# One core, one decoder block: the first loads merged and reordered, the row scale moved from the products to the down weight, and the last products reordered

## The chip, the core and the metric

The program runs on one core of one Trainium2 chip. The metric is the device time of one execution, in microseconds (us). The core has five engines that run side by side: TensorE (PE in the profile; PEld is its weight load), VectorE (DVE), ScalarE (ACT), GpSimd (POOL) and SyncE (SP), which here only issues DMA transfers. Data lies in SBUF (128 partitions); TensorE writes its sums to PSUM, here eight banks of 512 floats per partition.

## The reference

The input x is 4 batches of 256 tokens of 256 numbers. Three steps, each with a residual:

```python
x = x + linear_attention(layernorm(x))      # 16 heads of 16; q, k, v, o with biases; elu + 1
x = x + softmax_scores(ctx, ctx, layernorm(x), masks)   # (ctx Wq+bq)(ctx Wk+bk)^T/8 * layernorm(x), masked, softmax
x = x + ffn(layernorm(x))
# ffn:  y = fwht(x * SU_ug);  h = silu(y W_gate^T * ws_gate) * (y W_up^T * ws_up)
#       h = fwht(h * SU_dp);  out = h W_down^T * Wscale_dp
```

`fwht` is a normalised Hadamard transform over the last dimension; ctx is 4 x 256 x 64. The softmax of the second step is added to x itself, as its 256 columns are the 256 numbers of a token. `Wscale_dp` scales the 256 columns of the result, and since h W_down^T is linear in W_down, it can be put on the products or on the weight.

## The kernel before

**Tiles.** x lies in `x_res` (name `xs`) as 8 tiles of 128 tokens, two for each batch b. A factor that needs more than the short format of TensorE is split into a high part (a cast on ACT, functions `..._hi`) and a low part (a subtraction on DVE or POOL, `..._lo`), and one product is three passes: low by high, high by high, high by low.

**The start.** TensorE first runs `WARM` products of zeros (`junk`), then `mx` (the 65 x 65 product of the context weights), `u` (mx by the transposed context, in two halves), `T1` (the turn of the first batch's normalised x against the unit matrix), `SC` 0 (context scores of batch 0), and then K, V and Q of batch 0. The order is the list `HEAD`. x0 needs on its way to `T1`: statistics (`ln_stats` on DVE), `rstd_of` on POOL, `normalise1` on DVE; after `T1` comes `xT_hi` on ACT, at which K starts, and `xT_lo` on DVE. Each projection has a bias product of its own at its end; `bias_lo` on DVE makes the low part, and Q waits at its start for the second call.

**Masks.** The two masks' bytes are loaded, added on POOL (`mask_sum`), and spread to `mbias` on ACT (L396). The bytes lie in the buffer `at`, which `attend(0)` (L742) writes; `attend(0)` waits for `mbias` (L738).

**The feed-forward part.** For batch b and block j of 128 of the 1024 inner numbers, `gate_up` makes gate and up (L1123, 12 products); ACT takes silu (L521), DVE multiplies (`hidden`, L822), ACT and POOL split (L530, L311). `SIDE` says after which block of a batch the work for later batches is put in: `WD` 0 to 3 are the Hadamard products over the down weight, `XH` that over x. `down(b)` (L1136) sums both tiles of a batch over the eight blocks: first blocks 0 to 6 of tile 0, then of tile 1, then the last block of each. `add_y` on DVE scales the sum by `Wscale_dp` in PSUM (L833) and adds it to x (L835); SP then stores the tile.

**Banks.** Seven banks are handed out in turn, in the order of the groups. A group waits until its bank's last owner was read (`bank_read`). `XH` 1 takes the bank of `WD` 0, `GU` 6 that of `WD` 1, and the two sums of `down(0)` those of `WD` 2 and 3.

**Queues.** All loads but three are issued by SP in the order of the program, those three (context weights, unit matrix, bias rows) by ACT. Each engine does its own list strictly in order, and waits with the whole list behind it.

## Time and profile before

| | us |
|---|---|
| median of 3 runs | 138.21 |
| lowest, highest | 137.3, 138.31 |
| profiled execution | 135.21 |
| its span, first to last instruction | 133.4 |
| granted TensorE clock in it, mean | 0.998 |
| PE busy (share of the span) | 125.2 (94%) |
| DVE, ACT, POOL busy | 80.9, 75.8, 71.0 |

The profiled execution is 1.8 us longer than its span, and 3.0 us shorter than the median of the runs. All rows below are from it; times in them count from the start of the span. Instructions that read one list are read as: start, length, engine, line, operation, what it writes <- what it reads, how many; in brackets how long the engine was idle before it and what ended that.

### The profile page before, as it was taken

What the parts mean: (1) busy time and instruction counts of PE and PEld (TensorE: products, weight loads), DVE (VectorE), ACT (ScalarE), POOL (GpSimd) and SP (SyncE); (2) the same over time, 40 slices, a digit from 0 to 9 for tenths busy, and PEclk for the clock granted to TensorE, in tenths of its full rate; (3) what the DMA queues carried; (4) which work ended last, traced back from release to release, by engine and by line L of the source; (5) the groups of instructions that cost most, each with busy time, mean ns of one, the idle gap of its engine ahead of it and who ended that gap; (6) DMA issues with size and microseconds to landing.
All of it is one profiled execution on the core that took longest, in us unless ns stands there. A gap on an engine that the chain in (4) does not pass through costs nothing.

```text
span 133.4 us, 2624 instructions
## 1 busy us (share of the span) xinstructions
PE 125.2 (94%) x975; PEld 116.9 (88%) x975; DVE 80.9 (61%) x205; ACT 75.8 (57%) x162; POOL 71.0 (53%) x90
## 2 busy tenths in 40 slices
PE   6989797999899999999999999999999999999980
PEld 2249696999899999889999989999989999999980
DVE  0269985789986895857786696564635413324122
ACT  4168579595676589568543982654397530355300
POOL 3015999959999998855270352650226440144600
PEclk9999999999999999999999999999999999999999
DMA  3899976000000000000000200000200000200002
GB/s 69 231 387 374 396 244 227 5 0 2 2 5 0 0 2 5 0 0 0 5 0 0 79 0 5 2 0 0 82 1 0 2 0 5 79 0 0 5 0 79
DMA packets 4721, 7.64 MB, mean 57 GB/s; under 512 B 608, under 2 KB 2592, under 8 KB 4580
## 3 DMA queue, kind: packets, MB, share of 16 engines
q1 hardware_dynamic: 4478, 7.37, 16.1%
q10 hardware_dynamic: 230, 0.11, 0.5%
q8 instruction: 8, 0.13, 0.4%
q14 instruction: 5, 0.04, 0.1%
HBM read 6.42 MB, written 1.05 MB: 56 GB/s over the span
## 4 chain that ended last, share of the span: by engine, by line
PE 76%; DVE 6%; DMA 4%; SPq 3%; POOL 3%; ACT 2%; issue 2%; POOLq 0%; DVEq 0%
PE bank L1123 35%; PE bank L1136 17%; PE bank L1001 5%; PE bank L1087 4%; DMA at<-in_mask_key 4%; PE bank L1025 3%; PE bank L1109 3%; PE bank L1049 2%; PE bank L1059 2%; PE bank L1095 1%; PE bank L1069 1%; ACT mbias L396 1%; POOL at L280 1%; PE bank L992 1%; DVE st L647 1%
## 5 line engine op out<-in xcount | busy, mean ns | idle before, releaser
L1123 PE MATMUL bank<-xh_home,wug 128*128 128x256 f32 x384 | 49.5, 285 | 0.0
L1123 PEld LDWEIGHTS bank<-xh_home,wug 128*128 128x128 f32 x384 | 47.2, 190 | 0.5 <-issue 0.4
L311 POOL TENSOR_TENSOR hs<-front,hs 128x256 fp32r<-128x256 f32 x32 | 24.1, 761 | 32.6 <-ACT hs L530 32.6
L521 ACT ACTIVATE front<-bank,vecs 128x256 f32<-128x256 f32 x32 | 15.0, 473 | 18.6 <-PE bank L1123 18.5
L822 DVE SCALAR_TENSOR_TENSOR front<-bank,sc_up,front 128x256 f32<-128x256 f32 x32 | 15.2, 480 | 16.1 <-ACT front L521 16.1
L1136 PE MATMUL bank<-wdh,hs 128*128 128x256 f32 x192 | 23.8, 283 | 0.0
L1136 PEld LDWEIGHTS bank<-wdh,hs 128*128 128x128 f32 x192 | 23.4, 191 | 0.1
L530 ACT CAST hs<-front 128x256 fp32r<-128x256 f32 x32 | 12.8, 400 | 5.5 <-DVE front L822 5.4
L1025 PE MATMUL bank<-wqkv,xT 128*128 128x256 f32 x96 | 14.2, 289 | 0.0
L1025 PEld LDWEIGHTS bank<-wqkv,xT 128*128 128x128 f32 x96 | 12.3, 189 | 0.6 <-DVE xT L689 0.4
L647 DVE BATCH_NORM_STATS2 st<-x_res 128x6 f32<-128x256 f32 x24 | 9.1, 416 | 5.2 <-DMA x_res<-in_x 5.0
L258 POOL TENSOR_SCALAR veps<-mv 128x2 f32<-128x2 f32 x12 | 2.3, 193 | 16.0 <-DVE mv L650 15.3
L300 POOL TENSOR_TENSOR wd_b<-wd_a 128x1024 f32<-128x1024 f32 x4 | 10.0, 2509 | 0.1
L260 POOL TENSOR_TENSOR rstd<-veps,mhalf 128x2 f32<-128x2 f32 x12 | 8.5, 708 | 1.0
L833 DVE TENSOR_TENSOR bank<-bank,rows 128x256 f32<-128x256 f32 x8 | 3.4, 424 | 8.9 <-PE bank L1136 8.8
L1049 PE MATMUL bank<-xT,wqkv 128*128 128x256 f32 x48 | 7.1, 286 | 0.0
L1087 PE MATMUL bank<-wo,aT 128*128 128x256 f32 x48 | 6.5, 284 | 0.0
L1049 PEld LDWEIGHTS bank<-xT,wqkv 128*128 128x128 f32 x48 | 6.3, 190 | 0.0
L961 PE MATMUL bank<-back 128*128 128x512 bf16 x11 | 5.1, 629 | 1.3 <-POOL back L314 1.3
L1087 PEld LDWEIGHTS bank<-wo,aT 128*128 128x128 f32 x48 | 6.0, 190 | 0.0
L486 ACT ACTIVATE bank<-bank,low 128x256 f32<-128x256 f32 x8 | 3.6, 444 | 4.2 <-DVE low L775 4.2
L288 POOL TENSOR_TENSOR x_res<-x_res,rows 128x512 f32<-128x512 f32 x4 | 5.2, 1296 | 0.0
(105 smaller groups left out, 194.9 us busy)
## 6 DMA issues: line engine op xcount, KB each, us to landing
wd_a<-in_w_d SPq DMA_DIRECT2D x1, 1024.0 KB, 8.6
front<-in_w_ug SPq DMA_DIRECT2D x2, 512.0 KB, 9.8
back<-in_w_ug SPq DMA_DIRECT2D x2, 512.0 KB, 5.3
out<-x_res SPq DMA_DIRECT2D x8, 128.0 KB, 1.9
wd_b<-in_w_qkv SPq DMA_DIRECT2D x3, 256.0 KB, 5.6
x_res<-in_x SPq DMA_DIRECT2D x1, 512.0 KB, 6.8
back<-in_ctx_t SPq DMA_DIRECT2D x1, 260.0 KB
x_res<-in_x SPq DMA_DIRECT2D x2, 128.0 KB, 3.3
```

The costliest lines, as they stand in the source:

```text
L260: g.tensor_tensor(rstd[:, n - 1, two], veps[:, n - 1, two], mhalf[:, 0:2], ALU.pow).then_inc(s[f"rstd{n}"], 1)
L300: g.tensor_tensor(dst[:, :, half, :], src[:, :, 0, :], src[:, :, 1, :], ALU.subtract if half else ALU.add)\
L311: g.tensor_tensor(hs[:, 1, n % JB, :], sg[:, n % RING, :], hs[:, 0, n % JB, :].bitcast(F32), ALU.subtract)\
L521: a.activation(sg[:, n % RING, :], B("GU", n)[:, 0:SEQ], ACT.Silu, scale=vecs[:, V_WSUG + JB + j:V_WSUG + JB + j + 1]).then_inc(s["sg"], 1)
L530: a.copy(hs[:, 0, n % JB, :], sg[:, n % RING, :]).then_inc(s["h_hi"], 1)
L647: v.bn_stats(st[:, n - 1, t, :], xs[:, t, :]).then_inc(s[f"stats{n}"], 1)
L822: v.scalar_tensor_tensor(sg[:, n % RING, :], B("GU", n)[:, SEQ:2 * SEQ], sc_up[:, j:j + 1], sg[:, n % RING, :], ALU.mult, ALU.mult).then_i ...
L1025: ins = mm(into, xT[:, b % 2, xb, k, i * P:(i + 1) * P], wqkv[:, wa, c, k, :], start=(n == 0), stop=(name == "V" and n == len(X_PASSES) - 1))
L1049: mm(into, wqkv[:, wa, 2, k, m * P:(m + 1) * P], xT[:, b % 2, xb, k, :], start=(n == 0), stop=False)
L1087: ins = mm(dst[:, i * HID:(i + 1) * HID], aT[:, ab, k, i * P:(i + 1) * P], wo[:, wa, k, :], start=(n == 0), stop=(n == len(X_PASSES) - 1))
L1123: ins = mm(dst[:, n * SEQ:(n + 1) * SEQ], wug[:, wa, k, at_col + j * P:at_col + (j + 1) * P], xh[b][:, xb, k, :], start=(i == 0), stop=(i ...
L1136: ins = mm(dst[i][:, 0:HID], hs[:, hb, j, i * P:(i + 1) * P], wdh[:, wa, j, :], start=(j == 0 and n == 0), stop=(j == JB - 1 and n == 2))
```

## The change

The change has these parts:

- **First loads.** The unit matrix stands ahead of x in one array, and both share the buffer `x_res`; the first load brings it with both tiles of batch 0 (320 KB; before, two loads of 128 KB and one of 64 KB). The context weights stand behind the context in one array and come with it in the second load (293 KB, before 260 and 32.5 KB). The bias load on ACT's queue no longer waits for a memset on POOL. On SP's queue the row vectors and masks move up, and `vecs` moves down.
- **Bias rows.** Three rows instead of 65; they are negated, as is the row of ones that they are multiplied with.
- **Order at the start.** `WARM` is 8 instead of 9; `T1` comes between the two halves of `u`; `SC` 0 comes after Q. On ACT `xT_hi` and `exp_k` come earlier, on POOL `rstd_of(1, 1)` comes ahead of `ctx_lo(0)`, on DVE `xT_lo` comes ahead of `bias_lo` and `u_lo`, and `ln_stats(1, 1)` ahead of the second `bias_lo`.
- **Masks' bytes** lie in the buffer `score` instead of `at`. The wait of `attend(0)` for `mbias` stays in the code.
- **Down weight.** `wd_scale` on DVE multiplies the four `WD` groups by `Wscale_dp` in PSUM, ahead of `wd_hi` and `wd_lo`; `add_y` has one instruction per tile instead of two.
- **Last batch.** `down(3)` ends tile 0 after two blocks of tile 1; six blocks of tile 1 follow.

```diff
 BANKS = 8
-WARM, WARM_MORE = 9, 2
+WARM, WARM_MORE = 8, 2
...
-HEAD = (("mx", 0), ("u", 0), ("u", 1), ("T1", 0), ("SC", 0), ("K", 0), ("V", 0), ("Q", 0), ("T1", 1), ("ST", 0),
+HEAD = (("mx", 0), ("u", 0), ("T1", 0), ("u", 1), ("K", 0), ("V", 0), ("Q", 0), ("SC", 0), ("T1", 1), ("ST", 0),
...
-        xs = sb("x_res", [P, TILES, HID])
+
+        first = sb("x_res", [P, P + TILES * HID])
+        ident, xs = first[:, 0:P], first[:, P:].rearrange("p (t d) -> p t d", d=HID)
...
-        wx = sb("wx", [CTX, 2 * CTX1])
...
-        ctxT = back[0:CTX1, 0, :]
-        junk = back[:, 1, 0:CHUNK // 2].bitcast(BF16)
+        ctx_raw = back[0:CTX1, :, :].rearrange("p i c -> p (i c)")[:, 0:TOK + 2 * CTX1]
+        ctxT, wx = back[0:CTX1, 0, :], back[0:CTX, 1, 0:2 * CTX1]
...
-        bytes_of = at[:, :, :, :].rearrange("p two i d -> p (two i d)").bitcast(U8)
...
+        bytes_of = score[:, :, :].rearrange("p b s -> p (b s)").bitcast(U8)
...
         @block.sync
         def _(sp):
-            sp.dma_start(xs[:, 0:1, :], x[:, 0:1, :]).then_inc(ld["x0"], 16)
-            sp.dma_start(xs[:, 1:2, :], x[:, 1:2, :]).then_inc(ld["x1"], 16)
-            sp.dma_start(ctxT, ctx_t).then_inc(ld["ctx"], 16)
+            sp.dma_start(first[:, 0:P + ST * HID], x[:, 0:P + ST * HID]).then_inc(ld["x0"], 16)
+            sp.dma_start(ctx_raw, ctx_t).then_inc(ld["ctx"], 16)
             sp.dma_start(qkv_raw[:, 0], w_qkv[:, 0]).then_inc(ld["wk"], 16)
             sp.dma_start(qkv_raw[:, 1], w_qkv[:, 1]).then_inc(ld["wv"], 16)
             sp.dma_start(qkv_raw[:, 2], w_qkv[:, 2]).then_inc(ld["wq"], 16)
-            sp.dma_start(xs[:, 2:4, :], x[:, 2:4, :]).then_inc(ld["x2"], 16)
-            sp.dma_start(xs[:, 4:8, :], x[:, 4:8, :]).then_inc(ld["x3"], 16)
-            sp.dma_start(vecs[:, :], vec).then_inc(ld["vec"], 16)
+            sp.dma_start(first[:, P + ST * HID:P + 2 * ST * HID], x[:, P + ST * HID:P + 2 * ST * HID]).then_inc(ld["x1"], 16)
+            sp.dma_start(rows[:, 0:2, :], row[0:2, :].partition_broadcast(P)).then_inc(ld["row"], 16)
             sp.dma_start(mss, mask_ss).then_inc(ld["mss"], 16)
             sp.dma_start(mkey, mask_key.partition_broadcast(P)).then_inc(ld["mkey"], 16)
-            sp.dma_start(cst[:, P:], const[:, P:]).then_inc(ld["cst"], 16)
+            sp.dma_start(first[:, P + 2 * ST * HID:], x[:, P + 2 * ST * HID:]).then_inc(ld["x2"], 16)
+            sp.dma_start(cst[:, :], const).then_inc(ld["cst"], 16)
             sp.dma_start(wo_raw, w_o).then_inc(ld["wo"], 16)
-            sp.dma_start(rows[:, 0:2, :], row[0:2, :].partition_broadcast(P)).then_inc(ld["row"], 16)
+            sp.dma_start(vecs[:, :], vec).then_inc(ld["vec"], 16)
             sp.dma_start(wd_a[:, :, :], w_d).then_inc(ld["wd"], 16)
             for n, c in enumerate(UG_ORDER):
                 if n == 2:
                     sp.wait_ge(s["ctx_lo"], 2)
-                    wait_full(sp, "K", 0)
+                    wait_full(sp, "SC", 0)
                 sp.dma_start(stage[n], w_ug[:, :, c * CHUNK:(c + 1) * CHUNK]).then_inc(ld[f"ug{n}"], 16)
             sp.dma_start(rows[:, 2:3, :], row[2:3, :].partition_broadcast(P)).then_inc(ld["wsd"], 16)
...
             g.memset(junk, 0.0).then_inc(s["junk"], 1)
-            g.memset(bias_raw, 0.0).then_inc(s["bias_zero"], 1)
             g.memset(mhalf[:, :], -0.5)
...
             pool.wait_ge(s["xn1"], 2)
             mask_sum()
-            pool.wait_ge(s["w_lo"], 3)
-            ctx_lo(0)
             rstd_of(1, 1)
             shift_of(1, 1)
+            ctx_lo(0)
             ctx_lo(1)
             rstd_of(1, 2)
             shift_of(1, 2)
...
-            act.dma_start(wx[:, :], w_x).then_inc(ld["wx"], 16)
-            act.dma_start(cst[:, 0:P], const[:, 0:P]).then_inc(ld["ident"], 16)
+            act.dma_start(bias_home[:, 0:2 * HID + 1], bias).then_inc(ld["bias"], 16)
...
-                act.dma_start(bias_raw[ROW_HI:BIAS_ROWS:ROW_LO, :], bias).then_inc(ld["bias"], 16)
+            def minus_ones():
+                a.copy(minus[:, :], neg1[0:BIAS_ROWS, :].to_broadcast([BIAS_ROWS, HID])).then_inc(s["minus"], 1)
...
             def wd_hi(n):
-                wait_full(act, "WD", n)
+                act.wait_ge(s["wd"], n + 1)
...
-            bias_rows()
+            minus_ones()
             mx_copy()
             bias_hi(K_COLS)
             w_hi("wk", 0)
             u_copy()
+            xT_hi(0)
             u_hi(0)
-            xT_hi(0)
             w_hi("wv", 1)
             w_hi("wq", 2)
             bias_hi(Q_COLS)
+            exp_k(0)
             u_hi(1)
-            exp_k(0)
             ctx_hi(0)
             ctx_hi(1)
...
             def bias_lo(n, cols):
-                low_row = slice(ROW_LO, ROW_LO + 1)
+
                 dve.wait_ge(s["bias_hi"], n + 1)
-                v.tensor_tensor(bias_r[low_row, cols], bias_raw[low_row, cols], bias_r[low_row, cols].bitcast(F32), ALU.subtract)\
-                    .then_inc(s["bias"], 1)
+                v.scalar_tensor_tensor(bias_r[:, cols], bias_r[:, cols].bitcast(F32), bias_low, bias_raw[:, cols],
+                                       ALU.mult, ALU.subtract).then_inc(s["bias"], 1)
...
+            def wd_scale(n):
+
+                wait_full(dve, "WD", n)
+                if n == 0:
+                    dve.wait_ge(ld["wsd"], 16)
+                w = B("WD", n)[:, :].rearrange("p (j o) -> p j o", o=HID)
+                v.tensor_tensor(w, w, rows[:, 2:3, :].to_broadcast([P, WDP, HID]), ALU.mult).then_inc(s["wd"], 1)
...
             def add_y(b):
-
-                if b == 0:
-                    dve.wait_ge(ld["wsd"], 16)
                 for i in range(ST):
                     t = ST * b + i
                     wait_full(dve, "Y", b, i)
-                    y = B("Y", b, i)[:, 0:HID]
-                    v.tensor_tensor(y, y, rows[:, 2, :], ALU.mult).then_inc(s["y"], 1)
-                    dve.wait_ge(s["y"], t + 1)
-                    v.tensor_tensor(xs[:, t, :], y, xs[:, t, :], ALU.add).then_inc(read_of("Y", b, i), 1)
+                    v.tensor_tensor(xs[:, t, :], B("Y", b, i)[:, 0:HID], xs[:, t, :], ALU.add).then_inc(read_of("Y", b, i), 1)
 
             ln_stats(1, 0)
             normalise1(0)
             w_lo(0)
+            xT_lo(0)
             bias_lo(0, K_COLS)
             u_lo(0)
-            xT_lo(0)
             w_lo(1)
             w_lo(2)
+            ln_stats(1, 1)
             bias_lo(1, Q_COLS)
-            ln_stats(1, 1)
             elu_k(0)
             v_add(0)
             u_lo(1)
@@ -895,9 +894,13 @@
             hidden(2)
             x3_lo(1)
             hidden(3)
+            wd_scale(0)
+            wd_scale(1)
+            hidden(4)
             wd_lo(0)
             wd_lo(1)
-            hidden(4)
+            wd_scale(2)
+            wd_scale(3)
             at_lo(2)
...
-                pe.wait_ge(ld["wx"], 16)
+                pe.wait_ge(ld["ctx"], 16)
...
-                    pe.wait_ge(ld["ctx"], 16)
...
-                if b == 0:
-                    pe.wait_ge(ld["ident"], 16)
...
+                if b == BATCH - 1:
+
+                    for j in range(JB - 1):
+                        pe.wait_ge(s["h_lo"], JB * b + j + 1)
+                        block_products(0, j)
+                    block_products(1, 0)
+                    block_products(1, 1)
+                    pe.wait_ge(s["h_lo"], JB * b + JB)
+                    done(block_products(0, JB - 1), "Y", b, 0)
+                    for j in range(2, JB - 1):
+                        block_products(1, j)
+                    done(block_products(1, JB - 1), "Y", b, 1)
+                    return
...
-        "x": blocks(a["x"].reshape(TOK, HID)),
-        "ctx_t": np.concatenate([a["ctx_512"].reshape(TOK, CTX).T, np.ones((1, TOK), np.float32)]),
+        "x": np.concatenate([np.eye(P, dtype=np.float32), blocks(a["x"].reshape(TOK, HID)).reshape(P, -1)], 1),
+        "ctx_t": np.concatenate([np.concatenate([a["ctx_512"].reshape(TOK, CTX).T, np.ones((1, TOK), np.float32)]),
+                                 np.concatenate([w_x, np.zeros((1, 2 * CTX1), np.float32)])], 1),
         "w_qkv": np.stack([blocks(a[n].T) for n in ("L0_attn_k_w", "L0_attn_v_w", "L0_attn_q_w")], 1),
-        "bias": np.stack([b_kq, b_kq, np.ones(2 * HID, np.float32)]),
+        "bias": np.concatenate([np.stack([b_kq, b_kq, np.ones(2 * HID, np.float32)]), np.array([[0], [1], [0]], np.float32)], 1),
```

The change moves instructions in three places that matter here. **TensorE, from the start to the first K product**, before (bank: a PSUM bank; wx, mx, back, eq: context weights, their product, the home of the context, the first u; cst and x_res: where the unit matrix is):

```order
L961 MATMUL bank<-back 128x512 x9
L966 MATMUL bank<-wx 65x65
L961 MATMUL bank<-back 128x512 x2
L974 MATMUL bank<-back,mx 65x512 x2
L1001 MATMUL bank<-cst,xn 128x128 x4
L989 MATMUL bank<-eq,back 128x256 x2
L1025 MATMUL bank<-wqkv,xT 128x256 x6
L1031 MATMUL bank<-bias_r,ones 128x256
L1025 MATMUL bank<-wqkv,xT 128x256 x6
L1031 MATMUL bank<-bias_r,ones 128x256
```

And now:

```order
L964 MATMUL bank<-back 128x512 x8
L969 MATMUL bank<-back 65x65
L964 MATMUL bank<-back 128x512 x2
L976 MATMUL bank<-back,mx 65x512
L1003 MATMUL bank<-x_res,xn 128x128 x4
L976 MATMUL bank<-back,mx 65x512
L1025 MATMUL bank<-wqkv,xT 128x256 x6
L1031 MATMUL bank<-bias_r,minus 128x256
```

The two products of L989 (`SC` 0) are gone from here (they stand behind Q), one half of `u` stands behind the turn, and one warming product is left out.

**VectorE, from the first weight's low part to `elu_k(0)`**, before (wqkv: weights; hs here: the low part of u; st, mv: statistics of x):

```order
L685 TENSOR_TENSOR wqkv<-wd_b,wqkv 128x512
L661 TENSOR_TENSOR bias_r<-kvs,bias_r 1x256
L670 TENSOR_TENSOR hs<-bank,hs 65x256
L689 TENSOR_TENSOR xT<-bank,xT 128x512
L685 TENSOR_TENSOR wqkv<-wd_b,wqkv 128x512 x2
L661 TENSOR_TENSOR bias_r<-kvs,bias_r 1x256
L647 BN_STATS st<-x_res 128x6 x2
L650 BN_AGGR mv<-st 128x2 x2
L698 SCALAR_TENSOR_TENSOR kp<-ek,bank 128x512
```

And now:

```order
L682 TENSOR_TENSOR wqkv<-wd_b,wqkv 128x512
L686 TENSOR_TENSOR xT<-bank,xT 128x512
L658 SCALAR_TENSOR_TENSOR bias_r<-bias_r,kvs 3x256
L667 TENSOR_TENSOR hs<-bank,hs 65x256
L682 TENSOR_TENSOR wqkv<-wd_b,wqkv 128x512 x2
L644 BN_STATS st<-x_res 128x6 x2
L647 BN_AGGR mv<-st 128x2 x2
L658 SCALAR_TENSOR_TENSOR bias_r<-bias_r,kvs 3x256
L695 SCALAR_TENSOR_TENSOR kp<-ek,bank 128x512
```

The turned x comes first, and the statistics of the second batch stand ahead of the second bias row.

**VectorE in the first batch's feed-forward part, from `hidden(3)` on**, before (front: the hidden blocks; wdh: the split down weight; rows: the row vectors), with what each waits for:

```order
L822 SCALAR_TENSOR_TENSOR front<-bank,sc_up,front 128x256 [waits s_sg]
L813 SCALAR_TENSOR_TENSOR wdh<-bank,wdh 128x512 [waits s_wd_hi] x2
L822 SCALAR_TENSOR_TENSOR front<-bank,sc_up,front 128x256 [waits s_sg]
L679 TENSOR_TENSOR aT<-bank,aT 128x512 [waits s_at_hi]
L813 SCALAR_TENSOR_TENSOR wdh<-bank,wdh 128x512 [waits s_wd_hi] x2
L822 SCALAR_TENSOR_TENSOR front<-bank,sc_up,front 128x256 [waits s_sg]
```

And now:

```order
L827 SCALAR_TENSOR_TENSOR front<-bank,sc_up,front 128x256 [waits s_sg]
L813 TENSOR_TENSOR bank<-bank,rows 128x512 [waits ld_wsd,bank_full0]
L813 TENSOR_TENSOR bank<-bank,rows 128x512 [waits bank_full1]
L827 SCALAR_TENSOR_TENSOR front<-bank,sc_up,front 128x256 [waits s_sg]
L818 SCALAR_TENSOR_TENSOR wdh<-bank,wdh 128x512 [waits s_wd_hi] x2
L813 TENSOR_TENSOR bank<-bank,rows 128x512 [waits bank_full4]
L813 TENSOR_TENSOR bank<-bank,rows 128x512 [waits bank_full5]
L676 TENSOR_TENSOR aT<-bank,aT 128x512 [waits s_at_hi]
L818 SCALAR_TENSOR_TENSOR wdh<-bank,wdh 128x512 [waits s_wd_hi] x2
L827 SCALAR_TENSOR_TENSOR front<-bank,sc_up,front 128x256 [waits s_sg]
```

Four instructions on the banks of `WD` are new, and `hidden(4)` stands ahead of the first two low parts instead of behind them.

## Rows read from the trace of the kernel before

**Rows 1.** The waits of PE over the whole span: in total, times, longest, us.

```profile
PE bank L1001 <- DVE at L742: 1.1, 1, 1.1
```

**Rows 2.** Timeline, TensorE up to 11 us: start, length, what.

```profile
1.30 4.02 PE L961 MATMUL bank<-back 128*128 128x512 bf16 x9 [1.30 <-POOL back L314]
...
5.25 0.48 PE L966 MATMUL bank<-wx 64*65 64x65 f32 x2
5.66 1.03 PE L961 MATMUL bank<-back 128*128 128x512 bf16 x2
...
7.05 1.90 PE L974 MATMUL bank<-back,mx 65*65 65x512 f32 x4 [0.36 <-DMA back<-in_ctx_t]
...
8.79 0.60 PE L1001 MATMUL bank<-cst,xn 128*128 128x128 f32 x4
10.07 1.23 PE L1025 MATMUL bank<-wqkv,xT 128*128 128x256 f32 x6
```

**Rows 3.** Timeline, two DMA issues at the start.

```profile
0.72 0.57 ACTq L374 DMA_DIRECT2D wx<-in_w_x  x1
...
1.16 0.42 SPq L223 DMA_DIRECT2D x_res<-in_x  x1
```

**Rows 4.** DMA issues of the start; the last number is us to landing.

```profile
x_res<-in_x SPq DMA_DIRECT2D x1, 128.0 KB, 4.3
...
wx<-in_w_x ACTq DMA_DIRECT2D x1, 32.5 KB, 3.6
```

**Rows 5.** Timeline, VectorE and TensorE from 9 to 18 us.

```profile
9.15 0.41 DVE L661 TENSOR_TENSOR bias_r<-kvs,bias_r 1x256 fp32r<-1x256 f32 x1
...
10.05 0.69 DVE L689 TENSOR_TENSOR xT<-bank,xT 128x512 fp32r<-128x512 f32 x1
...
10.66 1.28 DVE L685 TENSOR_TENSOR wqkv<-wd_b,wqkv 128x512 fp32r<-128x512 f32 x2
...
11.97 0.84 DVE L661 TENSOR_TENSOR bias_r<-kvs,bias_r 1x256 fp32r<-1x256 f32 x1
...
13.52 0.88 PE L1049 MATMUL bank<-xT,wqkv 128*128 128x256 f32 x6
...
13.73 0.66 DVE L698 SCALAR_TENSOR_TENSOR kp<-ek,bank 128x512 f32<-128x512 f32 x1
...
16.27 0.84 PE L1001 MATMUL bank<-cst,xn 128*128 128x128 f32 x4 [0.91 <-ACT xn L432]
...
17.90 1.17 PE L1025 MATMUL bank<-wqkv,xT 128*128 128x256 f32 x6
```

**Rows 6.** Timeline, first batch's feed-forward stage, 58 to 64 us.

```profile
58.61 1.08 ACT L511 ACTIVATE wdh<-bank 128x512 fp32r<-128x512 f32 x2
...
59.23 1.29 DVE L813 SCALAR_TENSOR_TENSOR wdh<-bank,wdh 128x512 fp32r<-128x512 f32 x2 [0.97 <-ACT wdh L511]
59.98 1.20 PE L1109 MATMUL bank<-x3T,had_x 128*128 128x256 f32 x8
...
61.87 0.69 DVE L679 TENSOR_TENSOR aT<-bank,aT 128x512 fp32r<-128x512 f32 x1 [0.96 <-ACT aT L465]
...
63.67 0.47 DVE L822 SCALAR_TENSOR_TENSOR front<-bank,sc_up,front 128x256 f32<-128x256 f32 x1
```

**Rows 7.** Timeline, the turn of `at` 3 in the second batch's stage.

```profile
78.72 0.63 PE L1001 MATMUL bank<-cst,at 128*128 128x128 f32 x4 [0.26 <-issue]
```

**Rows 8.** The chain of waits, its step before the fourth batch's turn.

```profile
98.99 0.12 issue
```

**Rows 9.** Timeline, the end of the program.

```profile
123.72 5.92 PE L1136 MATMUL bank<-wdh,hs 128*128 128x256 f32 x48
...
124.77 1.44 POOL L311 TENSOR_TENSOR hs<-front,hs 128x256 fp32r<-128x256 f32 x2 [0.70 <-ACT hs L530]
...
129.32 0.43 DVE L833 TENSOR_TENSOR bank<-bank,rows 128x256 f32<-128x256 f32 x1 [4.41 <-PE bank L1136]
...
130.59 0.42 DVE L835 TENSOR_TENSOR x_res<-bank,x_res 128x256 f32<-128x256 f32 x1
```

More of the change, by code:

```diff
@@ L86, in schedule, with decoder_kernel @@
     return [g for g in order if g not in (("SC", 0, 0), ("SC", 1, 0))]
-def decoder_kernel(nc, x, ctx_t, w_qkv, bias, w_o, w_x, w_ug, w_d, vec, row, mask_ss, mask_key, const, out):
+def decoder_kernel(nc, x, ctx_t, w_qkv, bias, w_o, w_ug, w_d, vec, row, mask_ss, mask_key, const, out):
     bank_of, turn_of = {}, {}
@@ L113, in decoder_kernel @@
         bias_r = sb("bias_r", [BIAS_ROWS, 2 * HID], F32R)
-        ones = sb("ones", [BIAS_ROWS, HID], F32R)
-        cst = sb("cst", [P, 2 * P + FB * SW])
-        ident, had, diag_mask = cst[:, 0:P], cst[:, P:2 * P], cst[:, 2 * P:]
+        minus = sb("minus", [BIAS_ROWS, HID], F32R)
+        cst = sb("cst", [P, P + FB * SW])
+        had, diag_mask = cst[:, 0:P], cst[:, P:]
         mbias = sb("mbias", [P, TILES, SEQ], BF16)
```

31 lines of the change are left out of this document (14 added, 17 removed).

## The prediction

> **What bounds the kernel now.** I read the page first: TensorE is busy for 94% of the span and its clock stands at 1.00 on average, so a gain has to come from the start, from the few places where TensorE waits, or from what follows its last product. The list of waits by engine gives one wait in the middle of the first stage of 1.1 us, for `at` of the first batch [rows 1]. The timeline gives the others: before the warming products 1.30, before `u` 0.36, before the turn of the second batch 0.91 [rows 2, 5], before the turn of `at` 3 0.26, and 0.12 in the chain of waits at 98.99 [rows 7, 8]. After the last product come four instructions of VectorE and a store [rows 9]. About 1% (1.4 us) is what a measurement of this kernel can tell from no change.
>
> **First loads and the order of the start.** Let L be the landing of the load that brings the context and its weights. Now `mx` waits for it; before, `mx` had its own small load, and only `u` waited for the context, to 7.05 [rows 2]. From L on TensorE has `mx` 0.41 (5.25 to 5.66), two warming products 0.86, half of `u` 0.87 (7.05 to 8.79 is two), `T1` 0.44 (four of 128 columns at the cost per column of `u`), and the other half of `u` 0.87: K starts at L + 3.45. The other path to K, from the start of `T1` over `xT_hi`, took 1.28 (8.79 to 10.07) [rows 2] and is as long as `T1` and half a `u`, 1.31.
>
> L is in no row. From below: the small load of context weights landed 3.6 after its issue at 0.72, so 4.32. From above: the context alone ended the wait at 7.05. I take the load that stood second on SP's queue, as this one will: issued at 1.16, landed 4.3 later, at 5.46 [rows 2 to 4]. The new load is larger, but there is now one load in front of it on the queue and one beside it on ACT's, instead of three beside it. K then starts at 8.91 instead of 10.07. Of x I ask only that it land before the context, since it is ahead of it.
>
> The second load of the old queue speaks to a rule. It was 128 KB and took 4.3 us [rows 4]. The Trainium skill, DMA: Bandwidth & Descriptors, in the part on the fixed and the variable cost, gives about 2.0 us and the bytes at 436 GB/s, which is 2.3 us; the row disagrees by 2 us. By that rule both first loads together (613 KB) would have landed at about 4.2 us (an estimate from that page), K would start at 7.6, and the sum below would end 1.3 us lower.
>
> **From K to the second batch's turn.** Before, Q started 3.45 after K, and the turn 6.20 after K, of it 0.91 as a wait for the normalised x [rows 2, 5]. The reordered list of VectorE puts a wait ahead of Q: from `xT_lo`, which starts with K, come `xT_lo` 0.61, `bias_lo` and `u_lo` 0.90 (9.15 to 10.05), two `w_lo` 1.31 (to 11.97), the statistics of the second batch 0.92 (12.81 to 13.73) and `bias_lo` 0.46, sum 4.20 [rows 5]. Q waits at its start for that second `bias_lo`, so it starts 4.20 after K and not 3.45. Then come its 14 products at 0.12 (six in 0.88, of which the last one's length is 0.28), 1.68, and `SC` 0 at 0.87 (as many columns as half of `u`). The turn starts 6.75 after K, at 15.66, without a wait for x: the statistics end 3.7 after K, which leaves 3.0 for the way over POOL and ACT, and before it took 2.5 (13.73 to 16.27). Before it was 16.27. From the turn to the next K product I keep 1.63 (16.27 to 17.90), since `exp_q` waited for its place behind x before and waits for `SC` 0 now. **The start brings -0.61**; with L from 4.32 to 7.05 it is -1.75 to +0.98. The second `bias_lo` took 0.84 beside POOL's mask sum [rows 5]; if it does so again, 0.4 is lost.
>
> **Bias rows, queue order, warming product.** The bias products have as many columns as before and the low part as many elements per partition: nothing. The load of masks moves up two places on SP's queue, the scale vectors down by four, and they are read by VectorE only after 15 us; the load of the later halves of `w_ug` waits for `ctx_lo`, which now comes behind `rstd_of`, and for `SC` 0, and is not needed before the first feed-forward stage: nothing. The ninth warming product ended before 5.4, and TensorE would now wait for L anyway: nothing, unless its clock minds.
>
> **Masks' bytes.** They leave the buffer that `attend(0)` writes, but `attend(0)` still waits for `mbias`. The 1.1 us [rows 1] stay: nothing. The same edit with the wait gone would be worth up to that.
>
> **Down weight.** VectorE was free at 58.26 (0.97 before 59.23) and started `hidden(5)` at 63.67. Now it has eight instructions of 512 columns at 0.60 from start to start (one of `L813`'s pairs is 1.29 long with an overlap), `at_lo` 0.61 and `hidden(4)` 0.40, sum 5.81: `hidden(5)` starts at 64.07, 0.40 later. `XH` 1 takes the bank of `WD` 0 and waits for its low part, which now ends at 60.54 (58.26, two scales 1.20, `hidden(4)` 0.40, and the low part's own length 0.68), where TensorE was ready at about 60.14 (its row begins at 59.98, before the end of the product in front of it) [rows 6]. So TensorE loses 0.40 there, and VectorE's list is 0.40 late as well, which runs on through the scores of batch 2 to the turn of `at` 3 at 78.72, where TensorE already waits 0.26 for it [rows 7]: **+0.40**, once. If the scale hides, it is 0; if PSUM to PSUM is slower than that pair (0.68 and not 0.60 for four), +0.7.
>
> **`add_y`.** It loses one of two instructions per tile. In the first and third batch they stand where VectorE waits anyway: nothing. In the second they stand ahead of `ln_stats(3, 3)`, and 0.8 less there takes away the 0.12 [rows 8]: **-0.12**.
>
> **The end.** The last 48 products are the same number. Tile 0 now ends 18 products (18 x 0.12 = 2.2) before the last, so its sum and store are over before tile 1 is ready. The wait for the last low part comes after 27 products instead of 42, at 123.9 + 3.2 = 127.1; POOL had it at 126.2 [rows 9], so there is no new wait. Behind the last product stands one instruction of 0.42 instead of the chain from 129.32 to 131.01 (1.69): **-1.25** after 0.02 for the semaphore.
>
> **Sum.** -0.61 + 0.40 - 0.12 - 1.25 = -1.58, against the profiled 135.21: 133.6. The median of the runs is 3.0 above that execution; the terms carry over: 138.21 - 1.58 = **136.6**.
>
> **Rivals.**
>
> *The loads stream* (0.23). With one request on ACT's queue instead of three, the first loads come without a pause, and L is the 4.32 of the smallest load: 1.14 earlier, 135.5. For it: the second load's 4.3 us for 128 KB shows that bytes were not its limit. Against it: nothing shows what the limit was.
>
> *The context comes late* (0.14). L is 7.05 as before. Then `mx` and the warming products, which lay before it, lie behind it, and the start is 0.98 later instead of 0.61 earlier: 138.2, no change. For it: the load is 32 KB larger than the one that landed then.
>
> *TensorE is slow when the work comes* (0.19). The warming products took 4.02 for nine of 512 columns, 0.43 each, the 1.2 GHz level, though the clock column says 1.00; the two at 5.66 took 1.03, the same level; Q's took 0.12 for 256 columns, the 2.4 GHz level [rows 2, 5]. Before the rise the engine had been busy with a gap of less than 0.4. Now it works to 4.7 and then waits to L. The Trainium skill, TensorE: Matmul & The Clock Gate, Part 1, says that the engine starts throttled and that activity releases it; the rows agree. If the rise comes only after the second half of `u`, that costs 0.87 + 0.44 + 0.87 = 2.18, of which the wait of Q takes 0.7: 138.1 (0.08). If it comes after V, the 26 products of K and V take 0.21 instead of 0.12, 2.4 more: 136.6 + 2.18 + 2.4 - 0.7 = **140.5, slower** (0.11). It decides from the point where the clock is still low at K. For it: the runs of this kernel differ from the profiled one by 3 us. Against it: the same kind of activity is there, only with a gap of 0.8.
>
> **How the numbers follow.** The forecast has 0.44, with its own spread of 0.7 either way (the bias row's 0.4, the scale's 0 to 0.7); 1% below 138.21 is 136.83, which leaves 0.27 of it faster and 0.17 the same. Faster: 0.27 + 0.23 = 0.50. Same: 0.17 + 0.14 + 0.08 = 0.39. Slower: 0.11. The range goes from 135.2, the streaming loads with the scale partly hidden, to 138.9, the late context with the slower scale and bias row; outside lie the slow clock and a little of the streaming case.
>
> **What would show it.** The first K product at 8.9 (L + 3.45), Q held by `bias_lo` for 0.7, the second turn at 15.7 with no wait on ACT, `at` still held by `mbias`, `XH` 1 held by a `WD` low part for 0.4, tile 0's sum over before the last product, and 0.4 between the last product and the last store's issue. L above 6.1 or products of 256 columns at 0.21 after K has begun would make it wrong.

## The result: slower, and the profile after

| | before | after |
|---|---|---|
| median of 4 runs, us | 138.26 | 141.84 |
| lowest, highest | 137.3, 138.31 | 140.81, 142.29 |
| profiled execution, its span | 135.21, 133.4 | 142.07, 140.3 |

By the medians the changed kernel is 3.6 us (2.6%) slower. Over all its runs the kernel before has two groups of times, near 135.5 and near 138.5; the comparison takes the lower one, near 135.6, and so gives a ratio of 1.046 [1.042, 1.050]. The changed kernel has one group. The forecast was 136.6, faster.

The start in the timeline of TensorE, after:

```profile
1.29 3.59 PE L964 MATMUL bank<-back 128*128 128x512 bf16 x8 [1.29 <-POOL back L316]
5.42 0.48 PE L969 MATMUL bank<-back 64*65 64x65 f32 x2 [0.54 <-DMA back<-in_ctx_t]
...
6.66 1.92 PE L976 MATMUL bank<-back,mx 65*65 65x512 f32 x2
8.36 1.06 PE L1003 MATMUL bank<-x_res,xn 128*128 128x128 f32 x4
...
10.14 2.27 PE L1025 MATMUL bank<-wqkv,xT 128*128 128x256 f32 x6
...
12.85 1.65 PE L1025 MATMUL bank<-wqkv,xT 128*128 128x256 f32 x6
14.43 0.58 PE L1031 MATMUL bank<-bias_r,minus 3*128 3x256 f32 x1
...
19.58 0.98 PE L1049 MATMUL bank<-xT,wqkv 128*128 128x256 f32 x6
...
21.77 0.60 PE L1003 MATMUL bank<-x_res,xn 128*128 128x128 f32 x4
```

The load of context and weights ended the wait at 5.42, as forecast (5.46). But everything until 19.6 runs at the 1.2 GHz level: half of `u` took 1.7 (6.66 to 8.36), where two halves took 1.74 before [rows 2], and the second six of K take 1.58 (12.85 to 14.43) where six of Q took 0.72 before (13.52 [rows 5] to 14.24). TensorE does not wait once from 5.42 to 19.6: 14 us of unbroken products at the lower level. The clock column says 1.00 all the same (view by windows: the length of the stretch; busy time and, in brackets, number of instructions of PE, PEld, DVE, ACT and POOL; then clock, DMA share and GB/s):

```profile
6.00:10.00 4.00, 4.00 (x9) 1.78 (x8) 1.43 (x3) 1.87 (x6) 0.05 (x1) 1.00 1.05 276
```

In these 4 us TensorE was busy throughout with 9 products. K starts at 10.14 (before 10.07) and the second batch's turn at 21.77 (before 16.27).

The second thing is in the bias products, and it is there at the high clock as well. The chain of waits of the kernel before, K's products of a later batch (start, length, what):

```profile
40.07 0.12 PE bank L1031
40.20 0.72 PE bank L1025 x6
```

The same products in the chain of waits after:

```profile
47.43 0.31 PE bank L1031
47.74 0.90 PE bank L1025 x6
```

A bias product over 3 rows has the 256 columns of one over 65, and holds the engine for 0.31 instead of 0.12; the six behind it take 0.90 instead of 0.72. Where the 0.19 and the 0.18 come from, the weight loads show. Before (timeline of PEld, start and length of each load):

```profile
39.80 0.19 PEld L1031 LDWEIGHTS bank<-bias_r,ones 65*128 65x128 f32 x1
39.91 0.79 PEld L1025 LDWEIGHTS bank<-wqkv,xT 128*128 128x128 f32 x6
```

After:

```profile
47.36 0.18 PEld L1031 LDWEIGHTS bank<-bias_r,minus 3*128 3x128 f32 x1
47.67 0.77 PEld L1025 LDWEIGHTS bank<-wqkv,xT 128*128 128x128 f32 x6
```

The load is as long (0.18 against 0.19), but before it began 0.11 ahead of its product, at 39.91 in the timeline, under the product in front of it. After, it begins at 47.36 together with its own product's row, and the load of the product behind begins 0.31 later and not 0.11. The rows in front of the two loads end at 47.43 and 47.74, so by the profile, which models these ends, neither load lies under another product but for 0.07. The Trainium skill, TensorEngine Tiling (Array Packing), Key Properties, says that a change of the tiling mode, which that page ties to the number of rows (128, 64 or 32), drains TensorE; these rows agree with a drain on either side of the product over 3 rows, and do not show the mode itself.

Of the rest, the list of waits by engine says:

```profile
PE bank L1003 <- DVE at L739: 1.0, 1, 1.0
```

`attend(0)` still holds TensorE, as forecast (1.1 before [rows 1]). And the end of the chain of waits:

```profile
131.71 5.77 PE bank L1136 x48
...
137.51 0.42 DVE x_res L834
```

One instruction of 0.42 follows the last product, which ends at 137.48. Before, the chain of 1.69 [rows 9] did not start there. The chain of waits of the kernel before has, in front of it:

```profile
123.89 5.42 PE bank L1136 x45
```

VectorE started at 129.32, behind the 45th of the 48 products, when the sum of tile 0 was ready; the last product ended at 129.64 (126.72 and 2.92 in the timeline), and 1.37 stood behind it, up to 131.01. After, the same distance is 0.45 (137.48 to 137.93).

**The 6.9 us between the two spans, by stretches of the profiled executions:** to the first K product +0.07; from there to the turn of the second batch +5.43 (11.63 against 6.20: low clock and four bias products); to the first K product of the second batch +0.04; from there to the first gate product +3.29 (32.11 against 28.82: twelve bias products at the high clock); from there to the end -1.93 (84.75 against 86.68), where the forecast had +0.40 - 0.12 - 1.25 = -0.97.

### The profile page after: what moved, and what is told of

Same layout as the page of the kernel before. It is cut to its first block, busy times and chain, and to the rows that moved or that the text cites. A ratio compares the mean times of both kernels' runs of the same rounds, so it can differ in the third digit from the quotient of the medians.

```text
span 140.3 us, 2611 instructions
## 1 busy us (share of the span) xinstructions
PE 134.4 (96%) x974; PEld 122.6 (87%) x974; DVE 79.4 (57%) x201; ACT 76.0 (54%) x162; POOL 72.0 (51%) x89
## 4 chain that ended last, share of the span: by engine, by line
PE 90%; DMA 3%; ACT 3%; issue 1%; DVE 1%; SPq 0%; DVEq 0%; ACTq 0%
PE bank L1123 33%; PE bank L1136 16%; PE bank L1025 10%; PE bank L1049 5%; PE bank L1087 4%; PE bank L1003 4%; DMA back<-in_ctx_t 3%; PE bank L1109 3%; PE bank L976 2%; PE bank L1069 2%; PE bank L1059 2%; PE bank L1031 2%; PE bank L1050 2%; PE bank L994 2%; PE bank L1095 1%; ACT mbias L393 1%
## 5 line engine op out<-in xcount | busy, mean ns | idle before, releaser
L1025 PE MATMUL bank<-wqkv,xT 128*128 128x256 f32 x96 | 17.7, 334 | 0.1
L1025 PEld LDWEIGHTS bank<-wqkv,xT 128*128 128x128 f32 x96 | 14.6, 223 | 2.5 <-issue 1.3
L1049 PE MATMUL bank<-xT,wqkv 128*128 128x256 f32 x48 | 8.2, 309 | 0.0
L834 DVE TENSOR_TENSOR x_res<-bank,x_res 128x256 f32<-128x256 f32 x8 | 3.1, 419 | 8.8 <-PE bank L1136 8.7
L1049 PEld LDWEIGHTS bank<-xT,wqkv 128*128 128x128 f32 x48 | 6.8, 206 | 0.6 <-issue 0.2
L447 ACT ACTIVATE ek<-bank,neg 128x512 f32<-128x512 f32 x4 | 2.7, 687 | 7.4 <-PE bank L1031 7.4
L456 ACT ACTIVATE eq<-bank,neg 128x512 f32<-128x512 f32 x4 | 2.8, 690 | 6.4 <-PE bank L991 3.4
L964 PE MATMUL bank<-back 128*128 128x512 bf16 x10 | 4.6, 628 | 1.3 <-POOL back L316 1.3
```

What stands on the lines that cost most here:

```text
L1025: ins = mm(into, xT[:, b % 2, xb, k, i * P:(i + 1) * P], wqkv[:, wa, c, k, :], start=(n == 0), stop=(name == "V" and n == len(X_PASSES) - 1))
L1049: mm(into, wqkv[:, wa, 2, k, m * P:(m + 1) * P], xT[:, b % 2, xb, k, :], start=(n == 0), stop=False)
```

## The experiments

The theories. *Bias rows*: the product over 3 rows costs more in itself, against "columns alone count", on which the forecast rested. *Clock*: the first 20 us run at 1.2 GHz because of what TensorE does in the first five; within it, either the pause of 0.54 ahead of `mx` decides or the amount of work. The rest of the change is worth what the forecast said for it. All times are medians if nothing else is said, "before" stands for the kernel before on the same chip, and the medians of different groups come from different chips.

### First group: bias rows and warming, apart and together

Before here: 136.85 (135.33 to 139.38, 10 runs).

**a_bias65**: the change with its bias block zeroed to 65 rows, three of them loaded.

```diff
-BIAS_ROWS = 3
+BIAS_ROWS = 65
...
+            g.memset(bias_home[:, 0:2 * HID + 1], 0.0).then_inc(s["bias_zero"], 1)
...
+            act.wait_ge(s["bias_zero"], 1)
-            act.dma_start(bias_home[:, 0:2 * HID + 1], bias).then_inc(ld["bias"], 16)
+            act.dma_start(bias_home[0:3, 0:2 * HID + 1], bias).then_inc(ld["bias"], 16)
```

> The changed kernel with 65 bias rows instead of 3 (62 of them zeros, written by POOL ahead of the load). Theory R (a product over 3 rows takes 0.31 us and the one behind it 0.19 more, where 65 rows took 0.12): the pair of six products and a bias product falls from 1.11 to 0.84, 16 times 0.28 is 4.4 us, so the span falls from 140.3 to about 136. Theory C (the low clock alone explains the time, rows do not matter): no change.

Measured: 136.06 (132.65 to 136.87, 4 runs). Timeline of TensorE:

```profile
12.59 1.30 PE L1027 MATMUL bank<-wqkv,xT 128*128 128x256 f32 x6
13.72 0.28 PE L1033 MATMUL bank<-bias_r,minus 65*128 65x256 f32 x1
13.84 1.57 PE L1027 MATMUL bank<-wqkv,xT 128*128 128x256 f32 x12
```

At 65 rows the product holds the engine for 0.12 again (13.72 to 13.84). The clock is still late, rising within the six from 12.59 on. The times spread over 4 us: three runs took 135.5 to 136.9, and one 132.65, less than every run of a_bias65_warm10 below, so by its time the clock was early in it.

**a_warm10**: the change with ten warming products ahead of `mx`.

```diff
-WARM, WARM_MORE = 8, 2
+WARM, WARM_MORE = 10, 2
```

> The changed kernel with 10 warming products instead of 8, so that TensorE works until 5.5 us and the pause of 0.54 before the product of the context weights is gone. Theory C (that pause keeps the clock low until 19.6): halves of u at 0.87 instead of 1.71, K's products at 0.12 instead of 0.21, span 4 to 5 us lower, about 136. Rival (the moment of the rise is not tied to the pause): at most 0.2 us of difference, products at 0.21 still behind 15 us.

Measured: 136.37 (136.03 to 136.8, 6 runs), ratio 1.006 [1.003, 1.009]. Timeline of TensorE:

```profile
1.29 4.45 PE L964 MATMUL bank<-back 128*128 128x512 bf16 x10 [1.29 <-POOL back L316]
...
6.47 1.02 PE L976 MATMUL bank<-back,mx 65*65 65x512 f32 x2
7.33 0.60 PE L1003 MATMUL bank<-x_res,xn 128*128 128x128 f32 x4
...
8.60 1.23 PE L1025 MATMUL bank<-wqkv,xT 128*128 128x256 f32 x6
9.76 0.38 PE L1031 MATMUL bank<-bias_r,minus 3*128 3x256 f32 x1
10.08 0.97 PE L1025 MATMUL bank<-wqkv,xT 128*128 128x256 f32 x6
```

Half of `u` takes 0.86, the 2.4 GHz level, and K starts at 8.60. The ten products take 4.45 and `mx` follows without a pause. By the medians two more products of zeros bring 5.5 us, and one group of times. The bias product still takes 0.32 (9.76 to 10.08) and the six behind it 0.90.

**a_bias65_warm10**: both edits.

> Both: 65 bias rows and 10 warming products. R and C together: 131.5 to 132.5 of span, below the kernel before. R alone: as with 65 rows alone, about 136. C alone: as with 10 warming products alone.

Measured: 133.44 (133.24 to 133.72, 4 runs), ratio 0.985 [0.982, 0.988]: 1.5% below the kernel before. At 65 rows and early clock the parts of the change pay. The bias rows cost 136.37 - 133.44 = 2.9 where the clock is high, and 141.84 - 136.06 = 5.8 by the medians with eight warming products. Timeline of TensorE:

```profile
1.29 3.72 PE L966 MATMUL bank<-back 128*128 128x512 bf16 x10 [1.29 <-POOL back L316]
5.58 0.33 PE L971 MATMUL bank<-back 64*65 64x65 f32 x2 [0.57 <-DMA back<-in_ctx_t]
...
8.41 1.23 PE L1027 MATMUL bank<-wqkv,xT 128*128 128x256 f32 x6
...
12.35 0.94 PE L1051 MATMUL bank<-xT,wqkv 128*128 128x256 f32 x6 [0.22 <-issue]
...
15.65 0.84 PE L1005 MATMUL bank<-x_res,xn 128*128 128x128 f32 x4 [0.54 <-ACT xn L431]
```

Here a pause of 0.57 stands ahead of `mx`, as long as the 0.54 of the change, and the clock is high behind it. But it had risen before the pause: the ten products took 3.72, where the same ten took 4.45 in a_warm10.

**b_bias3**: the kernel before with the three bias rows of the change, and nothing else of it.

```diff
-ROW_HI, ROW_LO, ROW_ONE, BIAS_ROWS = 0, 32, 64, 65
+BIAS_ROWS = 3
...
```

> The kernel before with 3 bias rows (negated, with the row of -1 factors), nothing else changed. R: 4.4 us slower than before, ratio about 1.032. C or any other cause: within 0.3 us of before.

Measured: 141.5 (139.15 to 144.47, 4 runs), ratio 1.031 [1.023, 1.039]. By the medians this one part makes the old kernel 4.7 us slower, by the ratio 4.2. Its profiled execution (144.47) shows the low clock too:

```profile
7.56 3.65 PE L974 MATMUL bank<-back,mx 65*65 65x512 f32 x4 [0.87 <-DMA back<-in_ctx_t]
```

The same four products took 1.90 in [rows 2]; the work in front of them, nine warming products, `mx` and two more, is the same in both and took the same time. What differs is the pause behind it, 0.87 here and 0.36 there.

### Second group: what the other parts are worth

Here the base is a_bias65_warm10 (133.44), with high clock and 65 rows; before on this chip: 137.71 (135.3 to 139.66, 7 runs).

**m_free_at**: `attend(0)` no longer waits for `mbias` (the scores do, further on).

```diff
                 dve.wait_ge(s["z_inv"], b + 1)
-                if b == 0:
-                    dve.wait_ge(s["mbias"], 1)
```

> The kernel with 65 bias rows and 10 warming products, and with the wait of attend(0) for mbias taken out, which the move of the masks' bytes allows (at and the bytes share no memory any more). Theory M (the wait is all that held at): the wait of TensorE before the turn of at, 1.15 us in the kernel with both, falls to 0.4 or less, and the span by 0.7 to 1.1, to about 130.5. Rival (the wait only moves: logits(0) needs mbias too, and the chain through VectorE over the scores sets the time): the turn comes earlier, the span stays at 131.4 within 0.3.

Measured: 132.22 (131.94 to 132.71, 4 runs), ratio 0.972 [0.962, 0.983]; against the base -1.2, and -0.9 by the spans (130.5 and 131.4). The list of waits by engine no longer has the wait for `at`, 1.2 in the base. This is the fastest version of the study, 2.8% below the kernel before by the ratio and 4.0% by the medians of its chip. In the base, which has the masks' bytes moved and the wait kept, TensorE still waits 1.15; the move pays only with this line gone.

**m_old_tail**: the last batch summed in the old order.

```diff
-                if b == BATCH - 1:
-
-                    for j in range(JB - 1):
...
-                    done(block_products(1, JB - 1), "Y", b, 1)
-                    return
```

> The kernel with 65 bias rows and 10 warming products, with the last batch's products in the old order. Theory T: both tiles are ready together, and two additions of 0.42 stand behind the last product instead of one, so it is 0.4 us slower (the rest of the forecast 1.25 belongs to the scale that left add_y). Rival (the store of tile 0 delays that of tile 1 as well): 0.8 or more.

Measured: 133.25 (133.06 to 133.7, 4 runs), no difference to the base that these runs can tell, where 0.4 more was expected; the spans are 131.6 and 131.4. The end of the chain of waits:

```profile
122.86 5.42 PE bank L1138 x45
128.27 0.02 issue
128.29 0.78 DVE x_res L836 x2
```

And of the base:

```profile
122.89 5.77 PE bank L1138 x48
...
128.69 0.42 DVE x_res L836
```

In the old order VectorE starts behind the 45th product, in the new one behind the 48th. The two additions end at 129.07 and the one at 129.11. So with the scale on the weight the new order of the sums brings nothing.

**m_old_scale**: the scale back in `add_y`, the down weight unscaled.

```diff
-            wd_scale(0)
-            wd_scale(1)
-            hidden(4)
             wd_lo(0)
             wd_lo(1)
-            wd_scale(2)
-            wd_scale(3)
+            hidden(4)
             at_lo(2)
...
-                    v.tensor_tensor(xs[:, t, :], B("Y", b, i)[:, 0:HID], xs[:, t, :], ALU.add).then_inc(read_of("Y", b, i), 1)
+                    v.tensor_tensor(y, y, rows[:, 2, :], ALU.mult).then_inc(s["y"], 1)
+                    dve.wait_ge(s["y"], t + 1)
+                    v.tensor_tensor(xs[:, t, :], y, xs[:, t, :], ALU.add).then_inc(read_of("Y", b, i), 1)
```

> The kernel with 65 bias rows and 10 warming products, with the row scale in add_y as before and no wd_scale. Theory S (forecast): 0.45 more behind the last product, 0.3 to 0.4 less in the first batch's feed-forward part (XH 1 waits 0.3 in the kernel with both), 0.12 more before the fourth batch's turn: 0.2 slower, within 0.2. Rival (the four scales cost VectorE's chain 1 us or more): 0.5 faster or more.

Measured: 134.12 (133.56 to 134.42, 4 runs), 0.7 slower than the base, where 0.2 was expected; span 132.2. Chain of waits:

```profile
59.49 1.04 PE bank L1104 x8
...
98.31 0.12 issue
98.43 0.84 PE bank L998 x4
99.27 2.87 PE bank L1118 x24
...
129.00 0.44 DVE bank L831
...
129.47 0.43 DVE x_res L833
```

And the chain of waits of the base:

```profile
59.83 1.21 PE bank L1111 x8
...
98.53 0.44 PE bank L1005 x4
98.96 2.87 PE bank L1125 x24
```

Without the scale on the weight, `XH` 1 starts at 59.49 and without a wait, so the scale costs the base 0.34 there. At the turn of the fourth batch the base is 0.22 behind (98.53 against 98.31). Behind it the base is 0.31 ahead (98.96 against 99.27): the wait of 0.12 is gone, and the four products take 0.44 instead of 0.84. At the end (128.69 in the base) it is ahead by another instruction of 0.44 and its start.

**w_rows64**: the base with 64 bias rows, one run. 

> The kernel with both, but 64 bias rows. Question: from what number of rows does a bias product cost 0.12 instead of 0.31? If what counts is that the product uses less than the whole height, 64 rows would cost as 3 do (0.31, and 0.90 for the six behind it) and the span would be about 134.5; if only a height of at most 32 rows costs, it is 0.12 and the span 131.4.

Measured: 137.04, span 135.3, where 65 rows gave 131.4; K starts 0.6 later here (9.01 against 8.41), so 3.3 of the 3.9 lie behind it. By form, the bias products (busy, mean ns of one, idle) of w_rows64:

```profile
L1033 PE MATMUL bank<-bias_r,minus 64*128 64x256 f32 x8 | 3.0, 381 | 0.0
```

### Third group: the pause, the amount, and a better order

Before on this chip: 138.08 (135.24 to 139.79, 23 runs: 10 up to 135.9, 13 from 137.7 on).

**w_rows128**: the base with 128 bias rows, one run. 

> The kernel with 10 warming products and 128 bias rows: a bias product at 0.12 and 131.4 of span as with 65, if only products over at most 64 rows cost more. If the cost has a minimum near 65 rows, 0.2 or more per product.

Measured: 132.59, span 130.7. By form:

```profile
L1033 PE MATMUL bank<-bias_r,minus 128*128 128x256 f32 x8 | 2.3, 294 | 0.0
```

The chain of waits has the bias products at 0.31 in w_rows64 and at 0.12 here. With the change's 428 ns by form at 3 rows (part of them at the low clock) and 282 at 65 before, the price is not one of few rows as such: 64 rows pay it, 65 and 128 do not.

**a_more4**: the change with the eight products and the pause left, and four instead of two behind `mx`.

```diff
-WARM, WARM_MORE = 8, 2
+WARM, WARM_MORE = 8, 4
```

> The changed kernel (3 bias rows) with 8 warming products and 4 instead of 2 behind the product of the context weights: as many in all as with 10 and 2, but the pause of about 0.5 us after the first eight stays. Theory G (the pause decides whether the clock rises before u): as the changed kernel, 141 to 142, u's halves at 1.71. Rival N (the amount of early work decides): as with 10 warming products, 136.4, plus up to 0.9 where the two added products delay u.

Measured: 136.82 (136.23 to 142.64, 8 runs), ratio 1.007 [1.004, 1.009]. Two of the eight runs took 141.8 and 142.6, one 138.8. Timeline of TensorE:

```profile
1.30 3.19 PE L964 MATMUL bank<-back 128*128 128x512 bf16 x8 [1.30 <-POOL back L316]
5.61 0.33 PE L969 MATMUL bank<-back 64*65 64x65 f32 x2 [1.13 <-DMA back<-in_ctx_t]
```

The pause is 1.13 here, twice as long as in the change, and half of `u` takes 0.86 behind it. But the first eight products took 3.19, where the same eight took 3.59 in the change: the clock had risen within them, before the pause and before the two added products, which cannot have caused it. So this execution shows that a pause of 1.13 does not bring the clock down again once it has risen, and that the moment of the rise differs with the same work in front. Whether the added products help is left to the times: early in five of eight runs, against none of four of the change and one of four of a_bias65, which start in the same way. It is not enough to tell.

**b_warm11**: the kernel before with eleven warming products.

```diff
-WARM, WARM_MORE = 9, 2
+WARM, WARM_MORE = 11, 2
```

> The kernel before with 11 warming products instead of 9, so that TensorE works without a pause of over 0.2 us until u. Theory G or N: the clock has risen by u in every run, so the times of the kernel before, 135.3 to 139.7 so far, close up to 135.0 to 136.0. Rival (its spread comes from something else): the same spread as before.

Measured: 135.59 (135.34 to 136.32, 10 runs), ratio 1.001 [1.000, 1.003]. Nine of the ten runs lie in the lower group of the kernel before, up to 135.9, and the tenth is 0.4 above it; none is near the upper one. Its profile has a pause of 0.88 ahead of `u`, where none over 0.2 was expected; the clock had risen before it, within the eleven (4.21). So the 3 us by which the runs of the kernel before differ are the moment at which TensorE's clock rises, and eleven products settle it. The mean granted clock of each run agrees: 0.96 to 0.975 in 12 of the 13 runs of the upper group, 0.993 to 0.997 in the lower. No run of the upper group has a trace. The median gains 2.5 us.

**best2**: m_free_at with the statistics of the second batch behind the second `bias_lo` again, and on POOL `rstd_of(1, 1)` ahead of the sum of the masks.

```diff
-            mask_sum()
             rstd_of(1, 1)
             shift_of(1, 1)
+            mask_sum()
...
+            bias_lo(1, Q_COLS)
             ln_stats(1, 1)
-            bias_lo(1, Q_COLS)
```

> The best version by what was found: 65 bias rows, 10 warming products, at free of mbias, the second bias_lo ahead of the second batch's statistics, and rstd_of(1, 1) on POOL ahead of the mask sum. The wait of 0.5 before Q or before the second batch's turn goes: span 130.0, time 131.7, against 132.2 with at free alone. Rival (VectorE's chain over kp and the scores sets the time up to the first feed-forward part): 132.2 as with at free alone.

Measured: 133.37 (132.68 to 133.79, 6 runs), ratio 0.983 [0.978, 0.988]: not better than m_free_at, where 131.7 was expected. The second turn comes at 14.41 instead of 15.73, and nothing is left of it at the end. POOL (timeline of best2) shows where it went:

```profile
13.55 1.41 POOL L282 TENSOR_TENSOR score<-score 128x256 int32<-128x256 int32 x2
...
18.69 1.29 POOL L290 TENSOR_TENSOR x_res<-x_res,rows 128x512 f32<-128x512 f32 x1
19.94 2.38 POOL L302 TENSOR_TENSOR wd_b<-wd_a 128x1024 f32<-128x1024 f32 x1
```

From 12.3 to 31.7 POOL waits for no other engine, and the rstd of the next layernorms stands in its list behind these long instructions. TensorE was 1.3 earlier at 21 us and waited for the rest of it: 0.50 at 23.85, 0.43 at 31.78, 0.70 at 34.76 in its timeline. m_free_at has only 0.40 of these, at 34.22.

## Why the prediction was wrong

**The bias rows: "as many columns as before ... nothing". This step failed.** It counted columns and left out what stands around the product. At the high clock the group from the first bias product of a K to the next group's end (47.36 to 49.70 after, 39.91 to 41.58 before, same instructions) is 0.67 longer, 0.33 for each of two bias products; for 16 that is 5.4 on TensorE. Waits elsewhere take part of it: the twelve in the stretch from the second batch's K on cost 3.29, and all sixteen 2.9 by the medians at high clock (a_warm10 against a_bias65_warm10). The profiles of a_warm10 and a_bias65_warm10 agree: with 3 rows TensorE is busy for 129.2 and not 123.9, 5.3 more, and its waits behind the first are 2.3 less in sum (1.1 against 3.4). The rows before had one product over 64 rows between products over 128: `mx`, two of 65 columns, with no pause on either side [rows 2]. It took 0.41 (5.25 to 5.66), where the 130 columns would take 0.22 at the rate of `u` (1.74 for 2048 columns, doubled for the low clock). The forecast took over the 0.41 and did not ask what the rest was. Whether the rest is this price is not shown, but it was a reason to bound the cost.

**The ninth warming product: "nothing, unless its clock minds". It minds. This step failed too.** The rival "TensorE is slow when the work comes", in its severe form (140.5, chance 0.11), has the right mechanism: the clock was low at K and stayed so to 19.6. Its number came near by accident. With 65 rows the same eight products give 136.06 (a_bias65), since 138.21 already held most of the price; the rest of the 141.84 came with the bias rows. The rival's price was sized from rows, as 2.18 at the start and 2.4 in K and V. The runs give 5.5 with 3 rows (141.84 against 136.37), of which the kernel before pays 2.5 in its median already (138.08 against 135.59), since it loses the clock in more than half of its runs. The forecast subtracted its terms from the median, 138.21, without asking what the 3.0 above the profiled execution were; they were this term, and the change makes it larger. The two failed steps have in common that a term was put at nothing because no row was read as showing a cost.

**What decides the moment of the rise is not shown, but the 14 traces fall into three kinds.** In five (a_bias65_warm10, a_more4, b_warm11, w_rows128, best2) the clock rose within the first products, and pauses of up to 1.13 behind them did not matter. In six (before, a_warm10, m_free_at, m_old_tail, m_old_scale, w_rows64) it had not risen then, no pause was longer than 0.36, and it rose by 7.1. In three (the change 0.54, a_bias65 0.70, b_bias3 0.87) a longer pause came before the rise, and the clock then stayed low for 7 us or more of unbroken work. So the pause is the better of the two theories, together with a moment that differs from run to run, and more warming products ahead of the pause help in two ways: they shorten it, and they leave more time for the clock to rise before it. No run tests the pause apart from the amount of work.

**Whether the two failures feed each other is open.** With eight warming products, 3 rows instead of 65 cost 5.8 by the medians, and with ten 2.9; in the kernel before, 4.7 (141.5 against 136.85). In the profiled executions the clock rises at 12.5 with 65 rows and at 19.6 with 3, and seven microseconds of products at half speed are about 3.5. That the slow bias products themselves delay the rise would fit this, but was not shown apart from them: the one early run of a_bias65 lowers its median, and the execution of b_bias3 was already late before its first bias product, at 7.56.

**What held, and what was off in size.** The wait for the load of the context ended at 5.42 (forecast 5.46). The forecast took the landing of another load in the same place of the queue; the same wait ended at 5.52 to 5.90 in five other traces, and the 4.2 that the prediction also gives as an estimate was over 1 us too early. That the 4.3 of the second load speaks against the quoted 2.3 is only half of the record: the first load, of the same 128 KB, was issued at 0.72 and ended the wait of VectorE at 3.14 (timeline of the kernel before), 2.4 later. The Trainium skill, DMA: Bandwidth & Descriptors, Anatomy of one DMA, gives this rule for loads that GpSimd issues; these are issued by SP.

The rest is read from a_bias65_warm10, where the clock is high. K starts 2.83 after that wait's end (5.58 to 8.41) and not 3.45, because `mx` and the two warming products cost 0.26 and 0.44 there and not 0.41 and 0.86. Q starts 3.94 after K (forecast 4.20), and waits 0.22 by the profile. The turn comes at 15.65, where 15.66 was forecast, but that is luck: K is 0.5 and the way from K to Q 0.26 shorter than said, and against them stands above all a wait of 0.54 for the second batch's x, which the forecast called gone. The wait for `at` stayed, 1.0 to 1.2 (1.1). `XH` 1 waits 0.34 for the scaled weight (0.40), of which 0.22 reaches the fourth batch's turn. `add_y` was put at -0.12 there and is worth -0.53, since the forecast counted the wait and not that four products stretch from 0.44 to 0.84 behind one.

**The end was misread.** The forecast counted 1.69 behind the last product; 1.37 stood there, since the chain starts three products earlier. Now it is 0.45, so the term is -0.92 and not -1.25. And nearly all of it belongs to the scale: with the scale on the weight the old order ends as early (129.07 against 129.11). Only with the scale in `add_y` would the new order bring something, since there 0.93 stand behind the last product (128.97 to 129.90 in m_old_scale) instead of 1.37.

**The forecast's sum, at a high clock on both sides**, was -1.58; b_warm11 to a_bias65_warm10 is 135.59 to 133.44, -2.15, so the foreseen parts hold in sign and roughly in size. From before to after, the steps read: 138.26, less 2.5 for the clock of before, less 2.15 for the foreseen parts, 2.9 for the bias rows, 5.5 for the clock of after, 142.0. That this meets the measured 141.84 is no check: each step is a difference of the same medians, so the sum comes out by itself. The way the last two are shared out depends on their order, 2.9 and 5.5 or 2.6 (136.06 against 133.44) and 5.8.

## What to carry to other kernels

Before a product in a stream of others is made smaller, look at the products around it: the price here showed at two weight loads that no longer ran under another product, and it went away with zeros up to 65 rows. Where the runs of a kernel lie in two groups, find out what separates them before subtracting anything from the median; here two more products of zeros at the start brought 2.5 us before the change and 5.5 after it. Work brought forward only helps up to the next engine whose list is full: the 1.3 us won at the start of best2 ended in POOL's.

## What the runs showed of the hardware

- An fp32r product of 256 columns over 3 or 64 rows, between products over 128 rows, takes 0.31 from start to start where one over 65 or 128 rows takes 0.12, and the products behind it lose another 0.11 to 0.18 (47.36 to 49.70 in the change). By form the means are 381 ns at 64 rows, 282 to 297 at 65, 294 at 128. The length of the weight load stays the same (0.18 to 0.19). Why the load isn't hidden is not shown.
- The moment at which TensorE's clock rises differs from run to run of one kernel. With 8 or 9 warming products of 512 bf16 columns and 2 more behind `mx` it came late, by their times, in all four runs of the change, in three of four of a_bias65 and in 13 of 23 of the kernel before; with ten in the changed kernel (30 runs of eight versions) and 11 in the kernel before (10 runs) no run lies in a late group.
- TensorE can work for long at the 1.2 GHz level: without a pause from 5.42 to 19.6 in the change, and from 5.59 to 12.6 in a_bias65, before the clock rose. Once it had risen, a pause of 1.13 did not bring it down (a_more4).
- The clock column of the profile stood at 1.00 in a stretch in which every product ran at the 1.2 GHz level (6.00 to 10.00 in the change). The length of a product of known columns (256 in 0.21 or 0.12) told the two levels apart. In other runs it did show the low clock, as a mean of 0.96 to 0.975.
